# Reads of the first batch and the first down weights, issued earlier in the preparation's store queue

## The chip, the cores and the metric

One core of a Trainium2 chip runs the kernel. The metric is the device time of one execution in microseconds; the time before is the median of three runs. A batch is one of eight sequences of 512 tokens.

## What is computed

Each of 8 x 512 tokens of width 128 is normalised; a two-way state-space layer (forward and reversed, 256 channels, 16 states) and a mixture of 16 experts (the best 4 a token) are both computed from the normalised token and added to it. Cut to what matters:

```python
xn = _layernorm(x)
# state-space layer, for each direction
u = silu(causal_conv(x_part(xn)));  x_dbl = einsum('bdl,kd->bkl', u, xproj_w)
delta = softplus(dtproj(x_dbl[:, :r]) + dt_bias);  Bm, Cm = x_dbl[:, r:r+n], x_dbl[:, r+n:]
dA = exp(einsum('bdl,dn->bdln', delta, A));  dBx = einsum('bdl,bnl,bdl->bdln', delta, Bm, u)
h = associative_scan(a1*a2, a2*b1 + b2)          # along the sequence
y = (einsum('bdln,bnl->bdl', h, Cm) + Dp*u) * silu(z)
# experts
topv, topi = top_k(-dist2(xn, keys) + xn @ rw + rb, 4);  w = softmax(topv)
fused = sum_k w[k] * (gelu(xn @ w1[topi[k]] + b1) @ w2[topi[k]] + b2)
return x + out_proj(y_forward + y_backward) + fused
```

## The kernel before

The program has a start, a preparation and a main loop. Five engines run their own instruction lists and meet at semaphores.

The **preparation** goes through the eight batches. For each batch b, TensorE projects, ScalarE applies the activations, and VectorE does the convolution and the softplus; the results (delta, du = delta times u, gate, skip, parts, and the rows of C) are stored to DRAM, because all batches don't fit on the chip. Each result has one staging buffer, which the next batch writes again when the store has landed. GpSimd meanwhile scatters the token rows to the slots of their experts by 128 indirect DMAs (L804).

The **main loop** goes through the eight batches again, 32 steps (q) each. VectorE does a product (L1556) and two scans (L1568) a step, GpSimd multiplies the states by the rows of C (L838), TensorE fills PSUM banks with B (L1305, L1308), sums the states (L1244) and runs the experts' tiles; ScalarE makes the decays (L1068) and empties banks. A batch reads what the preparation stored: `early` is delta, du and parts, `late` is gate and skip. There are two places for each (par 0 and 1); batch 0 uses place 0, which the preparation doesn't use. The experts have a ring of two for their weights: w1 (up, `read_w1`) and w2 with b2 (down, `read_down`). The memory of w1 is also the staging buffer of the gate (`zg`), so it is free only when the last gate is stored; that of w2 is not used before.

SyncE (SP) issues all reads and stores, in the order of its program, so each one is issued only when all before it are. In the preparation that order is `store_prepared(b)` for b = 0 to 6: C of batch b+1, skip of b, gate of b+3, parts of b+1, delta of b, du of b, each after a wait for its writer. Then come `read_ahead` (L574: the early and the late reads of batch 0) and `read_weights` (L587: w1, w2 and b2 of the tiles 0 and 1, each after loading the tile's expert from the chip's memory, L551), then `store_prepared(7)` with skip, delta and du of the last batch, then `read_first` (L595: after the scatter has landed, the rows and tags of the tiles 0 and 1), a wait for `prepared`, and four reads of C rows (`read_c`, L654).

What the start of the main loop waits for: VectorE signals `prepared` (L1535) and goes on when the stores of gate, C, parts and delta of all eight batches have landed and du is made. TensorE waits for the last skip (`skip_sb`) and parts and for batch 0's early reads, then turns du (L1212) and B (L1217); ScalarE copies the results (L974), scales (L986) and makes decays, for which it waits for `decay_free` (VectorE's L1514); TensorE's first fills (L1305, L1308) follow. ScalarE copies skip to its staging buffer at L943, after TensorE's skip matmuls (L1185) and the landing of the store of the skip before. In step 1 TensorE turns the rows of tile 0 (L1258), and in step 0 GpSimd needs the first C rows.

Of the kernel before, what the change touches and what calls it, by code (L numbers as in the profile page):

```python
# [15 lines left out]
BATCH, L = 8, 512  # L16
# [39 lines left out]
W_RING = 2  # L56
# [202 lines left out]
PREP_STORES = ("gate_out", "c_out", "parts_out", "skip_out", "delta_out", "du_out")  # L259
# [34 lines left out]
def build_kernel(nc, x_in, consts_in, chan_in, inw_in, xproj_in, dtw_in, outw_in,  # L294
                 route_in, b2_in, w1_in, w2_in, out):
    with ExitStack() as ctx:
# [3 lines left out]
        def sem(name):  # L300
            return ctx.enter_context(nc.semaphore(name))
# [172 lines left out]
        s = {n: sem(n) for n in names.split()}  # L474
# [27 lines left out]
        def _(sp):  # L502
# [34 lines left out]
            def read_early(b, par, k):  # L537
                dst, src = early_reads(par)[k]
                sp.dma_start(dst, one(src, b)).then_inc(s[f"early_in{par}"], 16)

            def read_late(b, par, k):

                if k < NH:
                    sp.dma_start(gate[:, par, k, :, :], gate_d[bass.ds(b, 1)].rearrange("e p (t h c) -> (e p) h t c", t=TPB, h=NH)[:, k])\
                        .then_inc(s[f"late_in{par}"], 16)
                else:
                    sp.dma_start(skip[:, par, k - NH, :], skip_d[bass.ds(b, 1)].rearrange("e p (h l) -> (e p) h l", h=NH)[:, k - NH])\
                        .then_inc(s[f"skip_in{par}"], 16)

            def expert_of(tile):  # L550
                return sp.value_load(tile_expert[0:1, bass.ds(tile, 1)], min_val=0, max_val=E - 1)  # L551
# [4 lines left out]
            def read_w1(tile, slot):  # L556
                e = expert_of(tile)
                sp.dma_start(w1[:, slot, :], w1_in[bass.ds(e, 1)].rearrange("e p n -> (e p) n")).then_inc(w1_in_s[slot], 16)
# [9 lines left out]
            def read_down(tile, slot):  # L568
                e = expert_of(tile)
                sp.dma_start(w2[:, slot, :, :].rearrange("p f d -> p (f d)"),  # L570
                             w2_in[bass.ds(e, 1)].rearrange("e p n -> (e p) n")).then_inc(w2_in_s[slot], 16)
                sp.dma_start(b2[0:3, slot, :], b2_d[bass.ds(e, 1)].rearrange("e k d -> (e k) d")).then_inc(w2_in_s[slot], 16)

            def read_ahead():  # L574

                for n in PREP_STORES:
                    sp.wait_ge(s[n], 16)
                sp.wait_ge(s["slots_zeroed"], 16 * ZERO_DMAS)
                sp.wait_ge(s["acc_filled"], 16 * ACC_DMAS)
                for k in range(3):  # L580
                    read_early(0, 0, k)

                sp.wait_ge(s["gate_out"], 16 * BATCH)
                for k in range(2 * NH):
                    read_late(0, 0, k)

            def read_weights():  # L587

                sp.wait_ge(s["b2_out"], 16)
                sp.wait_ge(s["experts_ready"], 1)  # L590
                for j in range(W_RING):
                    read_w1(j, j)
                    read_down(j, j)

            def read_first():  # L595

# [23 lines left out]
            def store_prepared(b):  # L620
                if b + 1 < BATCH:
                    store_c(b + 1)
                store(b, skip_d, skip_p.rearrange("p h l -> p (h l)"), "skip_sb", "skip_out")
                if b + 3 < BATCH:
                    store_gate(b + 3)
                if b + 1 < BATCH:
                    store_parts(b + 1)
                store(b, delta_d, pos_part.rearrange("p q l -> p (q l)"), "delta_ready", "delta_out", ND)
                store(b, du_d, du_p.rearrange("p q l -> p (q l)"), "du_ready", "du_out", ND)
# [12 lines left out]
            store_gate(2)  # L642
            for b in range(BATCH - 1):
                store_prepared(b)
            read_ahead()
            read_weights()
            store_prepared(BATCH - 1)
            read_first()
            sp.wait_ge(s["prepared"], 1)
# [1039 lines left out]
```

## Time and profile before

| | us |
|---|---|
| median of 3 runs | 1097.3 |
| lowest and highest | 1092.97, 1101.39 |
| span of the profiled execution | 1105.0 |
| VectorE busy in it | 1030.1 (93%) |
| ScalarE busy | 940.6 (85%) |
| TensorE (matmul) busy | 932.6 (84%) |
| GpSimd busy | 909.1 (82%) |
| moved by DMA | 228.87 MB, mean 207 GB/s |

The span is that of one execution with the profiler on; it is 7.7 us above the median of the runs. Times in the rows count from the span's start. In a timeline a row with xN is N instructions merged, from the first one's start, with their time in all; in brackets stands how long the engine was idle before it and what ended that. "issue" there means that the profile found no releaser, "remote" that the releasing event belongs to no instruction it knows. The ends of matmuls are modelled.

### The profile page before, as it was taken

The numbers are of one execution on the slowest core, as the hardware profiler recorded it, in microseconds if no ns is written. First come the engines' busy times: TensorE is split into PE (matmuls) and PEld (weight loads), VectorE is DVE, ScalarE is ACT, GpSimd is POOL, SyncE is SP. The second block draws the span as 40 slices with busy tenths as digits, with TensorE's granted clock in tenths as the row PEclk, the third lists the DMA queues.
The fourth block names the chain that finished last, engine by engine and source line by source line (L and its number), as shares of the span: only waits on it lengthen the run. The fifth ranks groups of instructions, "written<-read, shape, count | busy, mean of one in ns | idle before, by whom it ended". The sixth has DMA issues, their size and how long they took to land.

```text
span 1105.0 us, 21807 instructions
## 1 busy us (share of the span) xinstructions
PE 932.6 (84%) x5794; PEld 735.3 (67%) x5866; DVE 1030.1 (93%) x1361; ACT 940.6 (85%) x1755; POOL 909.1 (82%) x567
## 2 busy tenths in 40 slices
PE   4569889955789898999998989989889989988894
PEld 2133333324678787878887877878778878877783
DVE  7789999777999999999999999999999999988897
ACT  3247999968899989999998999999989989988960
POOL 4178888863679999999999899989999999989762
PEclk9778888677999999999999999999999999998997
DMA  9945655689556767687778767776876787666668
GB/s 306 371 147 204 249 197 187 254 282 309 169 166 172 215 193 212 175 238 195 187 201 212 203 166 211 195 208 174 233 200 178 210 216 203 161 171 164 174 137 240
DMA packets 153108, 228.87 MB, mean 207 GB/s; under 512 B 36301, under 2 KB 98029, under 8 KB 147701
## 3 DMA queue, kind: packets, MB, share of 16 engines
q1 hardware_dynamic: 125844, 208.39, 58.6%
q0 software_dynamic: 27136, 19.02, 12.3%
q8 instruction: 51, 0.84, 0.3%
q14 instruction: 77, 0.62, 0.2%
HBM read 161.84 MB, written 69.64 MB: 209 GB/s over the span
## 4 chain that ended last, share of the span: by engine, by line
POOL 34%; issue 30%; ACT 14%; PE 10%; DVE 6%; DMA 3%; SPq 2%; POOLq 1%; ACTq 0%; DVEq 0%; another core or an unknown queue 0%
POOL arena L838 19%; POOL acc_d L823 14%; ACT arena L1068 3%; PE ps L1176 2%; PE ps L1160 2%; ACT arena L986 1%; DMA acc_d<-yrows,tags 1%; PE ps L1145 1%; ACT arena L1007 1%; DVE arena L1464 1%; ACT arena L937 1%; ACT arena L933 1%; ACT arena L1036 1%; PE ps L1244 1%; PE ps L1273 1%
## 5 line engine op out<-in xcount | busy, mean ns | idle before, releaser
L1568 DVE TENSOR_TENSOR_SCAN arena<-arena,ps 128x512 f32<-128x512 f32 x512 | 599.0, 1205 | 1.8 <-issue 0.8
L838 POOL TENSOR_TENSOR arena<-arena 128x1024 f32<-128x1024 f32 x246 | 527.2, 2469 | 54.6 <-DVE arena L1568 34.9
L1068 ACT ACTIVATE arena<-delta,a_neg 128x511 f32<-128x511 f32 x512 | 341.3, 728 | 2.6 <-DVE arena L1568 2.4
L823 POOL DMA_INDIRECT acc_d<-yrows,tags x160 | 252.7, 1579 | 45.2 <-issue 37.1
L1244 PE MATMUL ps<-ident,arena 128*128 128x128 f32 x2048 | 270.2, 275 | 4.6 <-DVE arena L1576 3.4
L1556 DVE TENSOR_TENSOR ps<-du,ps 128x512 f32<-128x512 f32 x352 | 233.2, 679 | 25.9 <-issue 9.5
L1244 PEld LDWEIGHTS ps<-ident,arena 128*128 128x128 f32 x2048 | 232.9, 142 | 15.1 <-DVE arena L1576 3.8
L804 POOL DMA_INDIRECT slots_d<-arena,pos x128 | 149.2, 1165 | 40.2 <-issue 35.8
L1273 PE MATMUL ps<-w,arena 128*128 128x128 f32 x1248 | 173.9, 282 | 3.4 <-ACT arena L1036 3.0
L1273 PEld LDWEIGHTS ps<-w,arena 128*128 128x128 f32 x1248 | 153.7, 192 | 12.8 <-issue 3.8
L1265 PE MATMUL ps<-rowsT,w 128*128 128x256 f32 x640 | 154.7, 385 | 7.8 <-ACT arena L1018 7.5
L986 ACT ACTIVATE arena<-arena 128x256 f32<-128x256 f32 x320 | 145.5, 511 | 0.0
L1265 PEld LDWEIGHTS ps<-rowsT,w 128*128 128x128 f32 x640 | 119.0, 193 | 26.7 <-ACT arena L1018 9.1
L1007 ACT ACTIVATE arena<-ps,w 128x256 f32<-128x256 f32 x312 | 123.8, 477 | 7.2 <-PE ps L1265 6.4
L1305 PE MATMUL ps<-ident,arena 128*128 128x128 f32 x640 | 95.0, 278 | 19.8 <-DVE arena L1568 16.0
L1305 PEld LDWEIGHTS ps<-ident,arena 128*128 128x128 f32 x640 | 74.3, 143 | 25.1 <-DVE arena L1568 18.0
L1013 ACT ACTIVATE yrows<-ps,tags 128x128 f32<-128x128 f32 x160 | 49.8, 365 | 46.7 <-PE ps L1275 21.0
L1036 ACT ACTIVATE arena<-arena 128x1024 f32<-128x1024 f32 x78 | 79.1, 1054 | 0.2
L1464 DVE SCALAR_TENSOR_TENSOR arena<-arena,chan 128x512 f32<-128x512 f32 x96 | 64.7, 742 | 0.0
L1258 PE MATMUL ps<-ident,rows 128*128 128x128 f32 x160 | 33.5, 291 | 36.6 <-ACT arena L1007 22.3
L1160 PE MATMUL ps<-arena 128*104 128x512 f32 x64 | 48.8, 934 | 5.3 <-DVE arena L1523 5.3
L1258 PEld LDWEIGHTS ps<-ident,rows 128*128 128x128 f32 x160 | 18.3, 142 | 51.9 <-ACT arena L1007 22.0
(154 smaller groups left out, 915.2 us busy)
## 6 DMA issues: line engine op xcount, KB each, us to landing
arena<-c_d SPq DMA_DIRECT2D x128, 512.0 KB
w<-w_dram SPq DMA_DIRECT2D x80, 258.0 KB
w<-w_dram SPq DMA_DIRECT2D x80, 256.0 KB
rows<-slots_d SPq DMA_DIRECT2D x80, 130.0 KB
slots_d<-delta SPq DMA_DIRECT2D x5, 2015.0 KB, 18.7
delta_d<-arena SPq DMA_DIRECT2D x8, 1024.0 KB
du_d<-delta SPq DMA_DIRECT2D x8, 1024.0 KB
delta<-delta_d SPq DMA_DIRECT2D x8, 1024.0 KB, 6.6
```

What stands on the lines that cost most here:

```text
L804: pool.indirect_dma_start(slots_d, bass.IndirectOffsetOnAxis(ap=pos[:, t * TOPK + k:t * TOPK + k + 1], axis=0), xn[:, t, :], None).then_in ...
L823: pool.indirect_dma_start(acc_d[j % W_RING], bass.IndirectOffsetOnAxis(ap=tags[:, j, a, 0:1].bitcast(I32), axis=0), yrows[:, j % W_RING, a ...
L838: nc.gpsimd.tensor_tensor(state[:, q % H_RING], state[:, q % H_RING], c_rows[:, r % C_RING], ALU.mult).then_inc(s["prod_done"], 1)
L986: last = nc.scalar.activation(scaled_du[scaled_slot(g, j)][:, t, :], duT[:, par, t, :], ACT.Identity, scale=bT[:, par, t, n:n + 1])
L1007: last = nc.scalar.activation(hidden[hidden_slot(b, j)][:, c, :], bank[:, f * S:(f + 1) * S], ACT.Identity, bias=w1[:, j % W_RING, FF + c: ...
L1068: nc.scalar.activation(decay[:, q % DA_RING, j, lo:lo + L - 1], delta[:, par, dh, lo:lo + L - 1], ACT.Exp, scale=a_neg[:, dh, 2 * g + j:2 ...
L1244: last = nc.tensor.matmul(y_ps[:, h, t * P:(t + 1) * P], state[:, q % H_RING, j, t * P:(t + 1) * P], ident[:, :], is_transpose=True, start ...
L1265: last = nc.tensor.matmul(bank[:, f * S:(f + 1) * S], w1[:, slot, c * P:(c + 1) * P], rowsT[:, :], start=True, stop=True)
L1273: nc.tensor.matmul(bank[:, a * P:(a + 1) * P], kept[:, c, a * P:(a + 1) * P], w2[:, slot, c, :], start=c == 0, stop=False)
L1305: last = nc.tensor.transpose(bank[:, t * P:(t + 1) * P], scaled_du[scaled_slot(g, j)][:, t, h * P:(h + 1) * P], ident[:, :])
L1556: nc.vector.tensor_tensor(b_ps[:, ROW[q, j], j, :], du[:, par, q % DH, :], b_row, ALU.mult)\
L1568: nc.vector.tensor_tensor_scan(state[:, q % H_RING, j, way], decay[:, q % DA_RING, j, way], b_ps[:, ROW[q, j], j, way], 0.0, ALU.mult, ALU ...
```

## The change

The early reads of batch 0 are issued behind the stores of batch 1 (`store_prepared(1)`), the late reads behind those of batch 2, and the reads of the first two tiles' w2 and b2 behind those of batch 3. The two reads of w1 stay where they are, ahead of the stores of batch 7, with the wait for all gates in front of them. The waits in front of the reads are cut to what each needs. No read and no store is added or taken away.

```diff
             def read_ahead():
 
-                for n in PREP_STORES:
+                for n in ("parts_out", "delta_out", "du_out"):
                     sp.wait_ge(s[n], 16)
                 sp.wait_ge(s["slots_zeroed"], 16 * ZERO_DMAS)
                 sp.wait_ge(s["acc_filled"], 16 * ACC_DMAS)
                 for k in range(3):
                     read_early(0, 0, k)
 
-                sp.wait_ge(s["gate_out"], 16 * BATCH)
+            def read_behind():
+
+                sp.wait_ge(s["gate_out"], 16)
+                sp.wait_ge(s["skip_out"], 16)
                 for k in range(2 * NH):
                     read_late(0, 0, k)
 
-            def read_weights():
+            def read_down_weights():
 
                 sp.wait_ge(s["b2_out"], 16)
                 sp.wait_ge(s["experts_ready"], 1)
                 for j in range(W_RING):
+                    read_down(j, j)
+
+            def read_up_weights():
+
+                sp.wait_ge(s["gate_out"], 16 * BATCH)
+                for j in range(W_RING):
                     read_w1(j, j)
-                    read_down(j, j)
...
             for b in range(BATCH - 1):
                 store_prepared(b)
-            read_ahead()
-            read_weights()
+                if b == 1:
+                    read_ahead()
+                elif b == 2:
+                    read_behind()
+                elif b == 3:
+                    read_down_weights()
+            read_up_weights()
             store_prepared(BATCH - 1)
             read_first()
```

## Rows read from the trace of the kernel before

**Rows 1.** The page, shares of the chain that ended last, by engine.
```profile
POOL 34%; issue 30%; ACT 14%; PE 10%; DVE 6%; DMA 3%; SPq 2%; POOLq 1%; ACTq 0%; DVEq 0%; another core or an unknown queue 0%
```

**Rows 2.** Busy time by stretch: stretch, length, PE, PEld, DVE, ACT, POOL, clock, DMA share, GB/s.
```profile
60.00:251.00 191.00, 154.97 (x320) 62.92 (x320) 167.10 (x216) 152.85 (x167) 148.82 (x135) 0.80 0.60 218
258.00:1065.00 807.00, 721.04 (x5188) 634.94 (x5258) 782.60 (x868) 754.58 (x1522) 723.90 (x396) 0.99 0.72 195
```

**Rows 3.** Timeline of SP, 232 to 255 us: start, duration, line, operation, out<-in.
```profile
232.31 0.71 SPq L606 DMA_DIRECT2D du_d<-delta  x1
234.50 0.70 SPq L539 DMA_DIRECT2D delta<-delta_d  x1
...
252.00 0.35 SPq L606 DMA_DIRECT2D delta_d<-arena  x1
252.47 0.78 SPq L606 DMA_DIRECT2D du_d<-delta  x1
253.60 0.94 SPq L561 DMA_DIRECT2D rows<-slots_d  x1
```

**Rows 4.** The chain that ended last in order of time, where the main loop begins.
```profile
258.60 4.93 DMA arena<-c_d
...
263.69 2.56 POOL arena L838 x2
```

**Rows 5.** Timeline of DVE, 247 to 261 us.
```profile
247.19 2.35 DVE L1505 TENSOR_TENSOR delta<-arena 128x1024 f32<-128x1024 f32 x2
249.50 0.17 DVE L1514 MEMSET arena<- 128x2 f32 x8
257.74 0.70 DVE L1556 TENSOR_TENSOR ps<-du,ps 128x512 f32<-128x512 f32 x1 [8.07 <-issue]
258.35 2.33 DVE L1568 TENSOR_TENSOR_SCAN arena<-arena,ps 128x512 f32<-128x512 f32 x2
```

**Rows 6.** Timeline of PE, 232 to 255 us.
```profile
232.02 6.40 PE L1185 MATMUL ps<-arena 128*128 128x512 f32 x8
248.06 1.97 PE L1212 MATMUL ps<-ident,du 128*128 128x128 f32 x8 [9.65 <-ACT gatedT L943]
...
253.30 1.09 PE L1305 MATMUL ps<-ident,arena 128*128 128x128 f32 x4 [3.15 <-ACT arena L986]
```

**Rows 7.** Timeline of ACT, 235 to 257 us.
```profile
235.32 1.02 ACT L923 ACTIVATE arena<-ps 128x1024 f32<-128x1024 f32 x1 [3.10 <-remote]
...
240.45 1.14 ACT L937 ACTIVATE arena<-du,fit_bias 128x1024 f32<-128x1024 f32 x1
246.99 1.01 ACT L943 COPY gatedT<-ps 128x1024 f32<-128x1024 f32 x1 [5.40 <-remote]
...
253.06 3.76 ACT L1068 ACTIVATE arena<-delta,a_neg 128x511 f32<-128x511 f32 x6
```

**Rows 8.** Timeline of POOL, the last indirect DMA of the scatter.
```profile
243.29 0.96 POOL L804 DMA_INDIRECT slots_d<-arena,pos  x1 [0.31 <-issue]
```

**Rows 9.** Busy time by stretch, as in rows 2, before the main loop.
```profile
230.00:235.00 5.00, 5.00 (x8) 1.80 (x7) 2.30 (x3) 2.17 (x3) 4.09 (x4) 0.57 1.04 413
235.00:240.00 5.00, 3.41 (x5) 1.03 (x4) 1.10 (x2) 4.65 (x5) 3.78 (x5) 0.75 0.98 268
240.00:245.00 5.00, 0.00 (x0) 0.00 (x0) 4.69 (x5) 1.59 (x2) 3.34 (x4) 0.59 1.02 398
```

**Rows 10.** Timelines of SP, DVE and ACT in the middle of the preparation.
```profile
131.99 0.39 SPq L606 DMA_DIRECT2D delta_d<-arena  x1
142.59 0.33 SPq L614 DMA_DIRECT2D c_d<-arena  x1
...
140.71 1.21 DVE L1489 SCALAR_TENSOR_TENSOR arena<-arena,du 128x1024 f32<-128x1024 f32 x1
...
158.46 0.56 ACT L905 COPY arena<-ps 104x512 f32<-104x512 f32 x1
```

**Rows 11.** Busy time by stretch, as in rows 2, behind the stores of batch 1.
```profile
140.00:142.00 2.00, 0.94 (x3) 0.12 (x1) 1.92 (x3) 2.00 (x3) 1.70 (x2) 1.00 0.20 71
```

## The prediction

> **What bounds the kernel now.** I read first the busy time by stretch. In the main loop VectorE works 782.60 of 807 us, 97% [rows 2]; in the preparation from 60 us on it works 167.10 of 191 us. So the time is VectorE's two stages and what lies between them. The chain that ended last names GpSimd first, with 34% [rows 1], but in the main loop GpSimd works 723.90 of 807 us [rows 2] and takes what VectorE hands it, so both would have to move for the end to move.
>
> Between the stages is a gap. VectorE's timeline ends the preparation with L1514 at 249.50 + 0.17 = 249.67 and begins step 0 with the product L1556 at 257.74, 8.07 us later [rows 5]. The reader is to see there that nothing computes. The timeline of SP says what it waits for: delta of batch 7 is complete when L1505 starts at 247.19 [rows 5], but its store is issued at 252.00 [rows 3], since SP is held up with the reads of batch 0 from 234.50 and then the weights. `prepared` needs that store landed: 252.00 to 257.74 is 5.7 us, which fits. TensorE had the first fills ready before: its L1305 ran at 253.30 [rows 6], the second fill some 0.4 us behind its end, about 254.8. GpSimd's first product is at 263.69, released by C rows issued at 258.60 that took 4.93 us [rows 4]. So the landing of the last delta store sets VectorE's start, and SP's list sets GpSimd's.
>
> **The change part by part.** Stores, reads and bytes stay the same in number; SP's order changes.
>
> *Taken from 234 to 251 us:* the early reads (2 x 1024 KB + 256 KB = 2.36 MB), the late ones (4 x 256 KB = 1.05 MB), and w2 with b2 (0.52 MB). What stays ahead of the stores of batch 7 is two w1 reads, 0.53 MB. SP ends the stores of batch 6 with du at 232.31 + 0.71 = 233.0 [rows 3]; From there to 252.0 it issues 13 reads today (3 early, 4 late, 2 each of w1, w2 and b2), 1.5 us each. The two w1 reads are 3 us at that pace, and even at twice that, for the expert loads, it is free by 239 and waits for batch 7. Its stores then go out when they are ready: delta at about 247.4 instead of 252.00, du at 249.7 instead of 252.47.
>
> *Landing of that delta store.* 1.05 MB at the 413 GB/s of rows 9 is 2.5 us, the lower bound; the upper one is the 5.7 us of today, with the skip store and weights ahead of it. With nothing ahead, as the skip would have left earlier, I take 3.6, nearer the lower: landed at 251.0. VectorE also needs two decays for its first scan; these follow L1514 at 249.67 at 3.76 / 6 = 0.63 each [rows 7], about 251.0, where today's first scan is at 258.35. VectorE therefore starts at about 251.0 instead of 257.74: **6.7 us earlier** (4.6 with the upper bound, 7.3 with the lower, where the decays decide).
>
> The Trainium skill (DMA: Bandwidth & Descriptors, Anatomy of one DMA) gives each DMA a fixed cost of about 2.0 us beside its bytes. An estimate by that page is 2.0 + 2.5 = 4.5 us for this store instead of 3.6, a start at 251.9 and 5.8 us instead of 6.7. No row shows the store alone.
>
> *The other gate* is TensorE and ScalarE. From ScalarE's skip copy L943 at 246.99 to the second fill at 254.8 is 7.8 us [rows 6, 7]. That copy started late: ScalarE was free at 240.45 + 1.14 = 241.6, the skip matmuls' modelled end is 232.02 + 6.40 = 238.4, and yet it waited 5.40 us, to 246.99, for an event that the profile can't name. The like happened at 235.32 (3.10 us). Both lie where the DMA share is 0.98 to 1.04 [rows 9]. If the reads' traffic causes the second, it goes with them: copy at 241.6, second fill at 249.4, no gate. If it stays, fills come at 254.8 as today, and the gain is 257.74 - 254.8 = **2.9 us**.
>
> *The runs against the profiled execution.* Its span is 1105.0, 7.7 above the median and 3.6 above the slowest run. The two nameless waits are 8.5 us together, so the timed runs may lack them. Without them in either kernel VectorE ends the preparation 3.1 us earlier, at 246.6. In the kernel before, the DMAs then set the landing: from 230 us on 2.10 MB of stores of batch 6, 2.36 + 1.05 + 1.05 MB of reads, and 1.57 MB of skip and delta of batch 7 are 8.1 MB, at the 413 GB/s of the first window 19.7 us, at the mean of rows 9 (360) 22.6: landed at 249.8 to 252.7, middle 251.2. In the changed kernel: delta issued at 244.3, landed at 247.9. Gain **3.3 us** (1.9 to 4.8).
>
> Three states of one mechanism give 2.9, 3.3 and 6.7. I take 4.5, between, as I can't tell which state a timed run is in: 1097.3 - 4.5 = **1092.8**. Against the profiled execution it would be 1105.0 - 6.7 = 1098.3.
>
> *Does the gain reach the end?* GpSimd must come too. SP issues du at 249.7, then four reads of rows and tags, at 1.2 us each today (253.60 to 258.60 [rows 3, 4]) or 0.5 where the queue is short: C rows issued at 252 to 255 instead of 258.60, landed 4.9 later, at 257 to 260 instead of 263.5. Its lag behind VectorE is 5.95 us today and 6 to 9 then; over the 256 steps VectorE needs 3.06 a step and GpSimd 2.83 [rows 2], and VectorE has eight state buffers (24 us) before it feels the lag. Rows of tile 0, needed in step 1, are issued 4.1 us ahead of VectorE's start today and 1.0 then, but behind 1.05 MB of stores instead of 2.62, which at 413 GB/s is 3.8 us less. I count no loss for them; the bound is the 3.1. The last indirect DMA of the scatter starts at 243.29 [rows 8]; SP asks for it at 250, so that wait is free up to a landing of 6 us. From there the main loop is the same work.
>
> *Added to the preparation:* at 133 us, behind du of batch 1, 2.36 MB; at 154, behind batch 2, 1.05 MB; at 175, behind batch 3, 0.52 MB with two expert loads. SP has nothing to issue from there to the next C store, 142.59 for the first [rows 10], and the new waits are for stores of batch 0, landed long before. The cover is idle DMA time: at 140 to 142 us the share is 0.20 [rows 11]. Gate, parts, delta and du of batch 1 and the reads are 5.2 MB, 12.7 us at 413 and 14.6 at 360; counted from the delta store at 131.99, with all of it still to come, they drain by 144.7 to 146.6. The C store of 142.59 is held up by up to 4 us; its buffer is written again at 158.46 [rows 10]. The tightest is delta of batch 1: issued at 131.99, landed 5.7 later at 137.7, awaited at 140.71 [rows 10], 3.0 us to spare. The reads stand behind it; were the engines to share evenly, it would take another 2.5 us and still be in time. Cost: nothing; without that cover, 0 to 2 us.
>
> **The rivals.**
> 1. *Nothing arrives.* Something else behind the start takes it: the rows, or the C rows for GpSimd, which only gain 3.6 of it at their upper cost. For it: the chain runs through GpSimd [rows 1, 4]. Against: VectorE's 97%. Time 1097.3, within 1.
> 2. *Both nameless waits are in the timed runs, and both go.* The preparation then also ends 3.1 earlier: 6.7 + 3.1 = 9.8, time 1087.5. Against: the first, at 235.32, is over before most of the reads are underway.
> 3. *The waits move with the reads (the slower side).* If reads of 3.4 MB beside running matmuls are what delays TensorE's release, it will happen at batch 2 and 3 instead, where VectorE has no idle time to hide it. Price: 3.1 + 8.6 (238.4 to 246.99) = 11.7, less 6.7: 5.0 slower, 1102.3. It decides once the waits put into the preparation pass 6.7 us. Against: the timelines of the middle of the preparation, where each batch's stores run beside the same matmuls, have no such wait.
>
> **How the numbers follow.** Forecast 0.70, rival 1 0.13, rival 2 0.08, rival 3 0.09. The forecast's own range is 1097.3 less 1.9 to 7.3: 1090.0 to 1095.4, and the median of three runs that spread from 1092.97 to 1101.39 is itself uncertain by some 3 us: 1087 to 1098.5. The range for 8 in 10 takes in rival 1 and part of 2: 1085 to 1100. A measurement here can tell about 1% from no change, 11 us. Faster by over that (below 1086.3) needs rival 2 and luck: 0.05. Slower by over that (above 1108.3) needs rival 3 at more than twice its price: 0.03. Within: 0.92.
>
> **What would show it.** Right: early reads at about 133 us; delta of batch 7 stored within 0.3 us of being ready; VectorE's gap after L1514 down from 8.07 to 1 to 5 us; first C rows issued by 255; preparation ending at 246 to 250 as before; the main loop as long as before. Wrong: VectorE idle before L1489 or the convolution in batches 2 to 4 (stores landing late), L943 waiting for a nameless event there, the gap still 8 us, or GpSimd's lag growing until VectorE waits.

## The result, and the profile after

| | before | after |
|---|---|---|
| median of 20 runs, us | 1096.66 | 1092.11 |
| lowest and highest | 1092.97, 1101.44 | 1087.96, 1096.31 |
| ratio, 95% interval | | 0.995 [0.9936, 0.9963] |
| span of the profiled execution | 1105.0 | 1091.1 |
| idle between the stages (VectorE) | 8.07 | 2.02 |

The change makes the kernel about 5 us faster, 0.5%; the interval is clear of no change, though the step is under the 1% that the prediction set out to tell. The medians differ by 4.6 us, the ratio's interval is 4.1 to 7.0 us. The forecast was 1092.8.

Timeline of DVE after, 238 to 247 us (start, duration, line, operation, out<-in, idle before it and its releaser), where the preparation ends; lines have moved by 13, so it answers [rows 5]:

```profile
238.63 2.35 DVE L1518 TENSOR_TENSOR delta<-arena 128x1024 f32<-128x1024 f32 x2
240.93 0.17 DVE L1527 MEMSET arena<- 128x2 f32 x8
243.13 0.70 DVE L1569 TENSOR_TENSOR ps<-du,ps 128x512 f32<-128x512 f32 x1 [2.02 <-issue]
243.74 2.32 DVE L1581 TENSOR_TENSOR_SCAN arena<-arena,ps 128x512 f32<-128x512 f32 x2
```

The gap behind the memsets is 2.02 us instead of 8.07. The releaser is the same unnamed one ("issue"). The timeline of SP after, 223 to 247 us, answers [rows 3]:

```profile
225.45 0.33 SPq L614 DMA_DIRECT2D du_d<-delta  x1
227.06 2.10 SPq L558 DMA_DIRECT2D w<-w_dram  x2
234.01 0.35 SPq L614 DMA_DIRECT2D skip_d<-gatedT  x1
238.81 0.35 SPq L614 DMA_DIRECT2D delta_d<-arena  x1
241.07 0.33 SPq L614 DMA_DIRECT2D du_d<-delta  x1
243.26 0.41 SPq L561 DMA_DIRECT2D rows<-slots_d  x1
```

SP is free from 229.2 us and waits for its writers. Delta's last write ended at 238.7, its store is issued at 238.81. The view of the DMAs issued from 238.5 to 239.5 us (KB, us from issue to landing) says when it is down:

```profile
delta_d<-arena SPq DMA_DIRECT2D x1, 1024.0 KB, 3.9
```

238.81 + 3.9 = 242.7, and VectorE goes on at 243.13. The main loop is as long as before, by stretches of 807 us from the first product on (columns of [rows 2]):

```profile
60.00:243.00 183.00, 146.60 (x326) 60.85 (x325) 162.16 (x210) 155.90 (x175) 144.90 (x132) 0.85 0.65 236
243.00:1050.00 807.00, 728.26 (x5262) 635.11 (x5263) 783.29 (x868) 757.13 (x1528) 723.72 (x396) 0.99 0.73 196
```

VectorE works 783.29 of 807 us, against 782.60 in [rows 2]. From first product to end it is 1091.1 - 243.13 = 848.0 us, against 1105.0 - 257.74 = 847.3. (Over the twelve executions below this stretch took 842.6 us in ballast_b to 851.3 in stores_first_b, and 844.2 in reads_twice, whose start is that of before. One profile thus can't show a gain of a few us at the end; the timed ratios have to.)

The two spans differ by 13.9 us, three times what the runs show, and only 6.05 of it is the gap. The rest lies in the execution of before that was profiled; a second one, below, has a span of 1095.2.

### The profile page after: what moved, and what is told of

Same layout as the page of the kernel before. It is cut to its first block and busy times, and to the rows that moved or that the text cites. A ratio compares the mean times of both kernels' runs of the same rounds, so it can differ in the third digit from the quotient of the medians.

```text
span 1091.1 us, 21878 instructions
## 1 busy us (share of the span) xinstructions
PE 932.0 (85%) x5866; PEld 732.8 (67%) x5866; DVE 1029.2 (94%) x1361; ACT 940.0 (86%) x1755; POOL 907.3 (83%) x567
## 5 line engine op out<-in xcount | busy, mean ns | idle before, releaser
L1321 PE MATMUL ps<-parts,sel 128*128 128x512 bf16 x176 | 59.3, 390 | 12.9 <-DVE arena L1581 12.9
```

## The experiments

Each row of the table is one kernel. Gain is 1097 times one less the ratio. "Ready" is the end of delta's last write by VectorE, "landing" the time from issue to landing of batch 7's delta store, "gap" VectorE's idle time ahead of its first product, "next 60" its idle time in the 60 us from that product on; all are from the profiled execution. For the kernels called split it is the second half of that store, whose issue is the end of SP's merged row for both less 0.33.

| kernel | ready | issued | landing | landed | VectorE starts | gap | next 60 | ratio [95%] | gain us |
|---|---|---|---|---|---|---|---|---|---|
| before_again | 237.6 | 241.37 | 6.1 | 247.5 | 247.86 | 7.87 | 0.5 | 0.9989 [0.997, 1.0008] | 1.2 |
| reads_twice | 239.0 | 242.01 | 7.1 | 249.1 | 249.50 | 8.02 | 0.5 | 0.9997 [0.9972, 1.0021] | 0.3 |
| ballast_b | 238.9 | 242.02 | 7.8 | 249.8 | 250.19 | 8.89 | 0.5 | 0.9998 [0.9976, 1.002] | 0.2 |
| stores_first | 241.7 | 241.80 | 6.7 | 248.5 | 248.87 | 4.78 | 1.5 | 0.9994 [0.9969, 1.002] | 0.7 |
| stores_first_b | 238.7 | 238.83 | 6.6 | 245.4 | 245.85 | 4.73 | 3.7 | 0.9994 [0.9975, 1.0013] | 0.7 |
| rest_alone | 239.1 | 239.18 | 5.9 | 245.1 | 245.83 | 4.34 | 1.7 | 0.997 [0.995, 0.999] | 3.3 |
| ballast_behind | 239.3 | 239.35 | 4.9 | 244.3 | 244.67 | 3.02 | 3.9 | 0.9985 [0.9967, 1.0003] | 1.6 |
| early_alone | 238.0 | 238.11 | 4.7 | 242.8 | 243.16 | 2.70 | 0.0 | 0.9951 [0.993, 0.9972] | 5.4 |
| after | 238.7 | 238.81 | 3.9 | 242.7 | 243.13 | 2.02 | 0.5 | 0.995 [0.9936, 0.9963] | 5.5 |
| after_again | 239.2 | 239.26 | 3.9 | 243.2 | 243.57 | 1.95 | 1.9 | 0.9918 [0.9889, 0.9946] | 9.0 |
| split (second half) | 242.2 | 242.26 | 2.7 | 245.0 | 245.35 | 0.78 | 0.5 | 0.9932 [0.9903, 0.9961] | 7.5 |
| split_b (second half) | 240.2 | 240.31 | 2.7 | 243.0 | 243.37 | 0.76 | 0.1 | 0.9946 [0.9924, 0.9968] | 5.9 |

ballast, which has no row here for want of a usable profile, is told below. In eleven of the twelve VectorE starts 0.4 us behind that landing, whatever else was moved. The exception is rest_alone with 0.7. The gap is thus three terms: how late the store is issued, how long it takes to land, and some 0.4 us, less the 2.3 to 2.4 us that VectorE still works behind delta's last write (for before_again 3.8 + 6.1 + 0.4 - 2.4 = 7.9). The expectations on record were written before these landings were read, and speak of a second gate at TensorE that this table leaves little room for.

The gap alone doesn't tell the gain; the gap and the next 60 us together do. Windows of DVE from the first product on, in before_again, stores_first_b and ballast_behind (stretch, length, VectorE busy, clock, DMA share, GB/s):

```profile
247.86:307.86 60.00, 59.51 (x67) 0.88 0.64 204
```
```profile
245.85:305.85 60.00, 56.26 (x63) 0.85 0.68 213
```
```profile
244.67:304.67 60.00, 56.10 (x63) 0.81 0.67 222
```

Where the rows of tile 0 go out too late for VectorE's start, it loses up to 3.4 us there that before_again doesn't lose: TensorE waits for them (to 251.52 in ballast_behind, 251.58 in stores_first_b), and the fills of step 2 stand behind them in its list. Gap and next 60 together fall below those of before_again by 5.9 us in after, 5.7 in early_alone, 2.3 in rest_alone, 1.4 in ballast_behind, 2.1 and -0.1 in the two of stores_first, 7.1 and 7.5 in the two of split, and -0.1 and -1.0 in reads_twice and ballast_b. All lie inside the interval of the timed gain but after_again, with 4.5 against 9.0 (5.9 to 12.2, from six runs).

### The kernel before, profiled once more

No edit. It tells the nameless waits of [rows 7] apart from the kernel.

> The kernel before, unchanged, profiled and timed once more. It asks whether the trace of before was typical. Ratio 1.000 with an interval of about 0.0015 either way. Theory A (the reads' traffic delays TensorE's release): the wait ahead of the skip copy L943 is there again, 3 to 6 us with no releaser named. Theory B (those waits were of that one execution): TensorE's release comes with the matmuls' end, the copy starts by 0.5 us after ScalarE is free, and the idle time of VectorE after L1514 is by so much longer or the preparation's end earlier. By either, the gap before the main loop is 5 to 9 us and the last delta store is issued 3 to 6 us after delta is made.

The timelines of DVE, ACT and SP, 224 to 248 us:

```profile
231.81 0.99 ACT L943 COPY gatedT<-ps 128x1024 f32<-128x1024 f32 x1
...
239.81 0.17 DVE L1514 MEMSET arena<- 128x2 f32 x8
247.86 0.70 DVE L1556 TENSOR_TENSOR ps<-du,ps 128x512 f32<-128x512 f32 x1 [7.87 <-issue]
...
225.58 1.13 SPq L539 DMA_DIRECT2D parts<-parts_d  x1
226.75 2.25 SPq L544 DMA_DIRECT2D gate<-gate_d  x2
229.05 5.65 SPq L547 DMA_DIRECT2D skip<-skip_d  x2
235.82 0.36 SPq L558 DMA_DIRECT2D w<-w_dram  x1
...
241.37 0.35 SPq L606 DMA_DIRECT2D delta_d<-arena  x1
```

L943 runs without a wait, and so does what comes before it; none of the twelve profiles of the table has a wait of ScalarE or TensorE put down to "remote" between 60 us and the main loop. The 3.10 and 5.40 us were that one execution's, which has a third such wait, of 2.65 us, at 86.87. The gap is there all the same, 7.87 us. SP's list sets it: delta was ready at 237.6 and issued 3.8 us later, the reads ahead of it having taken SP from 224.7 on. And the early reads, issued by 226.7, land late; the timeline of PE, 225 to 245 us, shows what waits for them:

```profile
238.22 1.94 PE L1212 MATMUL ps<-ident,du 128*128 128x128 f32 x8 [7.66 <-DMA parts<-parts_d]
...
244.73 1.06 PE L1305 MATMUL ps<-ident,arena 128*128 128x128 f32 x4 [0.22 <-issue]
```

VectorE's first product needs the fill L1308 between the two of L1305, so TensorE is ready before the second L1305 at 244.73 has run, some 3 us ahead of VectorE's start at 247.86; it isn't what ends the gap here.

The head of the preparation differs too. L1489 of batch 2 starts at 133.19 here and at 140.71 in [rows 10]; in the other executions that can be read it was 133.7 to 138.4. So of 13.9 us between the first two spans, 6.35 are the head (140.71 - 134.36), 6.05 the gap, and 2.2 the stretch from there to the memset's end (108.96 - 106.74), where the nameless waits were; 0.7 went the other way in the main loop.

### Only the early reads moved

```diff
                 if b == 1:
                     read_ahead()
-                elif b == 2:
-                    read_behind()
-                elif b == 3:
-                    read_down_weights()
+            read_behind()
             read_up_weights()
+            read_down_weights()
```

> Only the early reads (2.36 MB) are issued behind the stores of batch 1; late reads, w1, w2 and b2 stay ahead of the last stores. Theory (what counts is how much stands ahead of the last delta store): of the 3.94 MB that the change moves, 60% are gone, so some 2.5 to 3 us of the 4.6 us, ratio 0.9975, and SP still issues ten transfers there. Rival (SP's issue time counts, not the bytes): three of eleven moved issues are gone, 1 to 1.5 us. Rival (early reads are what TensorE's turn of du waits for): nearly the whole 4.6 us, 0.995.

Gain 5.4 us (3.1 to 7.7), the whole of the change's. With only three of the reads gone SP is through its list in time, and delta is stored at 238.11, as soon as it is made. That is neither the theory's 2.5 to 3 us by bytes nor the rival's 1 to 1.5 by issues: without the 2.36 MB in front of them the other issues are shorter too (the two skip reads took SP 2.14 us instead of 5.65), and a lateness can't fall below nothing. The third figure, nearly the whole, came true, but not by its mechanism, since TensorE's turn of du was no gate in before_again. It lands 0.8 us later than in the changed kernel (4.7 against 3.9), with the weights' reads just ahead of it, which is the 0.7 us that the gap is longer.

### Only the late reads and the down weights moved

```diff
-                if b == 1:
-                    read_ahead()
-                elif b == 2:
+                if b == 2:
                     read_behind()
                 elif b == 3:
                     read_down_weights()
+            read_ahead()
             read_up_weights()
```

> The other half alone: the late reads behind the stores of batch 2, w2 and b2 behind those of batch 3, the early reads at their old place. By bytes 1.57 of 3.94 MB are gone, 1.8 us, ratio 0.998; by issues eight of eleven, 3 us or more, 0.997; if TensorE's turn of du waits for the early reads, 0.5 us at the most, 1.000.

Gain 3.3 us (1.1 to 5.5). The timelines of SP, PE with its weight loads (PEld), and DVE:

```profile
239.18 0.35 SPq L614 DMA_DIRECT2D delta_d<-arena  x1
...
239.00 1.94 PE L1224 MATMUL ps<-ident,du 128*128 128x128 f32 x8 [5.88 <-DMA parts<-parts_d]
...
244.88 0.15 PEld L1320 LDWEIGHTS ps<-parts,sel 128*128 128x128 bf16 x1
...
245.52 1.06 PE L1317 MATMUL ps<-ident,arena 128*128 128x128 f32 x4 [0.22 <-issue]
...
245.83 0.69 DVE L1568 TENSOR_TENSOR ps<-du,ps 128x512 f32<-128x512 f32 x1 [4.34 <-PE ps L1317]
```

Delta is issued on time here too, yet the gap is 4.34 us. The view of DMAs issued from 239 to 239.7 us says why: the store takes 5.9 us behind the 2.36 MB of early reads.

```profile
delta_d<-arena SPq DMA_DIRECT2D x1, 1024.0 KB, 5.9
```

Its landing would have let VectorE start at 245.1 + 0.4 = 245.5. It started at 245.83. The early reads also held up TensorE's turn of du, to 239.00, and with it the fill that the first product needs, L1320 (L1308 in the kernel before). Its weights are loaded at 244.88, its matmul is missing in the trace; where it is there, it stands 0.43 us ahead of the fill behind it and takes 0.63, so here it would be over at 245.52 - 0.43 + 0.63 = 245.7 (an estimate). So TensorE is the last gate in this kernel, by some 0.3 us. The gains of the two halves, 5.4 and 3.3, add up to more than the whole, 5.5: each takes away the same lateness of 3.8 us, and moving the early reads takes most of the longer landing as well.

### The order of before, with the last stores ahead of the weights

```diff
             read_ahead()
-            read_weights()
             store_prepared(BATCH - 1)
+            read_weights()
```

> Before's order but for one swap: the weights (w1, w2, b2 of the first two tiles) are read behind the stores of batch 7, not ahead of them. If the landing of the last delta store sets VectorE's start, it is issued within 0.5 us of delta's being made, and the gap after L1514 shrinks by 3 to 5 us; ratio 0.996 to 0.998, with the early and late reads in place. If the bytes already in the queue set the landing, not the issue, the gain is that of 1.05 MB, 2 to 2.5 us. If the main loop swallows an earlier start, 1.000. The weights arrive later; w1 is needed in step 3, some 9 us in, so it costs nothing.

> Before's order with the weights behind the stores of batch 7, once more. Its first profile had a gap of 4.8 us instead of 7.9, and from the middle of the preparation to the main loop 3.1 us less than before_again, but its timed ratio was 0.9994 with an interval from 0.9969 to 1.0020. If the gap is what counts, the ratio is 0.997; if rows and tags, which now stand behind the weights, cost what the start gains (VectorE waited 1.1 us in step 1 or 2), 0.998 to 1.000.

Both times the gap is 3.1 us shorter, and both times the gain is 0.7 us with no change inside its interval (-2.2 to 3.4, then -1.4 to 2.7). Two things are to be seen. First, DVE's timeline of stores_first_b names TensorE's fill for the gap; the timeline of PE has the fill that the product needs:

```profile
244.26 0.63 PE L1308 MATMUL ps<-parts,sel 128*128 128x512 bf16 x1
...
245.85 0.70 DVE L1556 TENSOR_TENSOR ps<-du,ps 128x512 f32<-128x512 f32 x1 [4.73 <-PE ps L1305]
```

The expectations took it at its word. But that fill was over at 244.89, 0.96 us ahead of the product, and those of L1305 are for the first scan and the next step. The delta store of 238.83 landed 6.6 us later, at 245.4, 0.4 us ahead of the product as everywhere else. So the name doesn't tell what came last (in split, below, neither).

Second, the 3.1 us aren't kept. The weights are now ahead of rows, tags and C rows. The timelines of SP, DVE and POOL:

```profile
238.83 0.34 SPq L606 DMA_DIRECT2D delta_d<-arena  x1
...
248.10 0.31 SPq L572 DMA_DIRECT2D b<-b_d  x1
248.78 0.41 SPq L561 DMA_DIRECT2D rows<-slots_d  x1
...
250.76 2.22 SPq L654 DMA_DIRECT2D arena<-c_d  x4
...
252.73 1.29 DVE L1556 TENSOR_TENSOR ps<-du,ps 128x512 f32<-128x512 f32 x2 [1.13 <-PE ps L1308]
...
256.26 5.91 POOL L838 TENSOR_TENSOR arena<-arena 128x1024 f32<-128x1024 f32 x3 [16.77 <-DMA arena<-c_d]
```

The first C rows go out 4.9 us behind VectorE's start, where before_again issued them at 247.80, 0.06 ahead of it; rows follow VectorE's start by 2.9 us instead of preceding it by 4.9. GpSimd begins 10.4 us behind VectorE. VectorE idles 3.7 us in the next 60 us, against 0.5 in before_again: the whole of the 3.1 us is spent there. In the profile of stores_first it is 1.5 us, which leaves 2.1; the main loop is longer by 4.0 and 1.0 us (851.3 and 848.3 against 847.3).

So the gain became a new wait, in one execution all of it, in the other a third.

### The reads of before made twice

All reads of the change are issued in the preparation (`read_besides`, behind the stores of batches 1, 2 and 3) and once more at their old place.

```diff
             for b in range(BATCH - 1):
                 store_prepared(b)
+                read_besides(b)
+            sp.wait_ge(s["extra"], 16 * 11)
             read_ahead()
```

> Before's order, and the 3.94 MB that the change moves are also read, into the same places, behind the stores of batches 1, 2 and 3; at their old place everything is read again. It costs the moved reads' presence in the preparation and leaves their old place as it was. Theory (idle DMA time covers them): ratio 1.000 within 0.0015, VectorE's rhythm of 21.1 us a batch unchanged there. Rival 3 of the prediction (the reads hold TensorE or a store up in mid-preparation): each batch that they touch gets longer, 3 to 8 us in all, ratio 1.003 to 1.007, with VectorE idle ahead of its convolution or of L1502.

Ratio 0.9997: 3.9 MB more in the middle of the preparation cost nothing that the runs can tell (-2.3 to 3.1 us). Timelines of DVE, the first instruction of this kind in batch 2 and in batch 3, in reads_twice, then in before_again and after:

```profile
134.57 1.22 DVE L1518 SCALAR_TENSOR_TENSOR arena<-arena,du 128x1024 f32<-128x1024 f32 x1
...
155.71 1.22 DVE L1518 SCALAR_TENSOR_TENSOR arena<-arena,du 128x1024 f32<-128x1024 f32 x1
```
```profile
133.19 1.21 DVE L1489 SCALAR_TENSOR_TENSOR arena<-arena,du 128x1024 f32<-128x1024 f32 x1
...
154.32 1.21 DVE L1489 SCALAR_TENSOR_TENSOR arena<-arena,du 128x1024 f32<-128x1024 f32 x1
```
```profile
134.36 1.21 DVE L1502 SCALAR_TENSOR_TENSOR arena<-arena,du 128x1024 f32<-128x1024 f32 x1
...
155.48 1.22 DVE L1502 SCALAR_TENSOR_TENSOR arena<-arena,du 128x1024 f32<-128x1024 f32 x1
```

21.14, 21.13 and 21.12 us a batch. These rows reach as far as batch 3. The down weights come in behind it, but from the first of these instructions to the end of the memsets the preparation takes 106.9 us in reads_twice, 106.8 in before_again and 106.7 in after. Rival 3, that the waits move into the preparation, would have shown here.

### Reads put ahead of the last delta store, and behind it

Five reads, 1.31 MB together, into places that nothing needs, in the changed kernel: two halves of gate, two of skip, and parts, all to place 1.

```diff
+                if b == BATCH - 1:
...
+                    sp.dma_start(parts[:, 1, :, :].rearrange("p d l -> p (d l)"), one(parts_d, 0)).then_inc(s["extra"], 16)
                 store(b, delta_d, pos_part.rearrange("p q l -> p (q l)"), "delta_ready", "delta_out", ND)
```

> The changed kernel, with five reads (gate, skip and parts of batch 0 into the unused places, 1.31 MB) put right ahead of the last delta store once delta is made. The early reads are in since long, so TensorE's side is ready. If the landing of the delta store sets VectorE's start and the main loop passes it on: 1.31 MB at 410 GB/s, the landing 3.2 us later, gap 2.0 + 3.2 = 5.2 us, the time 3 to 4 us above the changed kernel's, ratio to before about 0.998. If only the early reads' landing counted, the gap stays 2 to 3 us and the ratio 0.995.

The profiled execution of this kernel took 4968.9 us, with TensorE at a fraction of its pace (1040 ns a matmul of the state sums, 275 in before), and says nothing on the gap. It wasn't every engine, as the next expectation has it: VectorE's scans took 1208 ns, in before 1205. Its timed runs gave 1.0025 [1.0001, 1.0049], 2.7 us slower than before where 0.998 was expected. It was run again:

> The kernel of ballast once more (1.31 MB of reads right ahead of the last delta store of the changed kernel), since its profiled execution ran at a small fraction of the speed in every engine and can't be read. Its timed runs were about 8 us above the changed kernel's, not the 3 to 4 expected. Theory now: the DMA engines take 3.2 us for the bytes, and SP's five issues, at 0.5 to 1.2 us each in a filled queue, put the delta store itself 2.5 to 5 us later, so gap 2.0 + 5 to 8. Rival: the gap is 5 and the main loop itself is longer by 3 to 4, because rows, tags and C rows come later too.

> The same five reads behind the last delta store, ahead of that of du. Same bytes and issues, same delay for du, rows, tags and C rows, none for delta. If the landing of the delta store alone sets the start: gap 2.0 to 3 us and ratio 0.995, 5 us or more below ballast_b. If the lateness of rows and C rows is what costs: as ballast_b.

The same traffic ahead of the store takes the change's gain away (0.9998, after 1.0025 in ballast; gap 8.89); behind it, it leaves a gap of 3.02 us. The DMAs, first of ballast_b, then of ballast_behind:

```profile
delta_d<-arena SPq DMA_DIRECT2D x1, 1024.0 KB, 7.8
```
```profile
delta_d<-arena SPq DMA_DIRECT2D x1, 1024.0 KB, 4.9
```

Against after_again, the five reads ahead cost 3.0 us in lateness (issued 3.1 after ready instead of 0.1) and 3.9 in landing, 6.9 together, and the gap grew by 6.94. Behind the store only the landing grows, by 1.0, and the gap by 1.07. The gap of ballast_behind is 4.9 us below that of before_again, but the gain is only 1.6 us (-0.3 to 3.6; 0.9985 where 0.995 was expected). Of the difference 3.4 us are idle time in the next 60 us, most of it in step 2 of its DVE timeline, where a fill comes late:

```profile
252.67 1.29 DVE L1577 TENSOR_TENSOR ps<-du,ps 128x512 f32<-128x512 f32 x2 [2.25 <-PE ps L1329]
```

So late rows cost too, once the landing is out of the way: they are issued at 244.45 here, 0.2 us ahead of VectorE's first product. In ballast_b they are issued at 243.19, 7.0 us ahead of it, and nothing is lost behind the start.

### The changed kernel again, and a store in two halves

after_again has no edit. split stores delta and du of batch 7 in halves, each as soon as it is made:

```diff
+                    for d in range(ND):
+                        sp.wait_ge(s[ready], ND * b + d + 1)
+                        sp.dma_start(one(dst, b)[:, d * NH * L:(d + 1) * NH * L],
+                                     src[:, d * NH:(d + 1) * NH].rearrange("p q l -> p (q l)")).then_inc(s[stored], 16)
```

> The changed kernel once more, timed beside the others and profiled again. Ratio 0.995 as on record; gap after VectorE's last preparation instruction 2 to 3 us; from the first product of the main loop to the end 847 to 848 us, as in every trace so far.

> The changed kernel, with the last delta and du stored as two halves by direction, the first as soon as it is made (3.8 us ahead of the second). The second half is 0.52 MB instead of 1.05: its landing 1.2 us sooner, so the gap goes from 2.0 to 1.0 or less, where the two first decays (1.3 us behind the end of the preparation, first scan 0.6 us behind the product) take over: 0.8 to 1.2 us, ratio 0.994. That is about what an interval here can tell; the gap in the profile decides. If C rows for GpSimd were the bound, nothing.

> The changed kernel with the last delta and du stored in halves, once more. Its first profile had a gap of 0.8 us instead of 2.0, ended by TensorE's fill, with the ratio 0.9932 (0.9903 to 0.9961). Expected 0.993 to 0.995; it can't be told from the changed kernel by the interval, so the gap is read again: 0.8 to 1.3 us.

after_again has the gap of after (1.95 us) and the landing of after (3.9). In split the last DMA to wait for has half the size and lands in 2.7 us instead of 3.9, and the gap falls by the same 1.2, to 0.78 and 0.76. The profile names a fill of L1325 here too, but the one that the product needs, L1328, was over at 241.81 in split_b. DMAs of split_b, issued from 240.1 to 241.0 us, and its DVE timeline:

```profile
delta_d<-arena SPq DMA_DIRECT2D x1, 512.0 KB, 2.7
```
```profile
243.37 0.70 DVE L1576 TENSOR_TENSOR ps<-du,ps 128x512 f32<-128x512 f32 x1 [0.76 <-PE ps L1325]
```

Against before it is 0.9932 and 0.9946, gains of 7.5 and 5.9 us; the changed kernel had 0.995 and, from six runs, 0.9918. The 1.2 us are in the traces, twice; the runs can't tell them.

## Why the prediction was right

**The time.** 1092.8 forecast, 1092.11 measured, and the mechanism is the one named: batch 7's delta store was late in SP's list and late in landing, VectorE waited for it, and the main loop passes the gain on. But the 4.5 us were a middle of three figures, and two of those fell; that it came so near is in part luck.

**Landing of that delta store.** Predicted: 4.6 us less late, 3.6 to land instead of 5.7, 6.7 us in the profile. Measured between after and before_again: 3.7 less late, 3.9 to land instead of 6.1 (5.9 together), gap 2.02 instead of 7.87 (5.85), and 6.05 against the profile of before. Two terms were mis-sized: 3.6 was 3.9, and 0.4 us lie between the landing and VectorE's product, 4.3 in all. The estimate by the Trainium skill (DMA: Bandwidth & Descriptors, Anatomy of one DMA), 4.5 us and a gain of 5.8, came nearer than mine. That section gives its 2.0 us for DMAs issued from GpSimd, which the prediction doesn't say; this store is issued from SP. By the two sizes here, 1.05 MB landed in 3.9 us and 0.52 MB in 2.7, so 1.2 for half the bytes and 1.5 for the rest; counted to VectorE's product it is 4.3 and 3.1, and 1.9 for the rest, which agrees.

**The other gate.** This step failed. Its price of 2.9 us hung on the nameless 5.40 us at L943, taken for a delay of TensorE's release by the reads' traffic. before_again has the same reads and no such wait. What the reads do delay is TensorE's turn of du, by landing late themselves (L1212 at 238.22, 7.66 us idle), and their own share in the landing of the delta store. As a gate for VectorE it came last in one kernel alone, rest_alone, by some 0.3 us. Why TensorE's releases came late in the one execution stays open.

**The runs against the profiled execution.** This step failed too. It said that without the nameless waits the gap would be set by 8.1 MB of traffic and the gain be 3.3 us. before_again is that case, and its gap is 7.87 us: the delta store was still issued 3.8 us late. The sum took the span of before, 7.7 us above the median, for a sign of those waits; but 2.2 us of it were theirs and the larger part was a late head, older than batch 2. The figure for either state is therefore the same, about 6 us, and lies inside the runs' 4.1 to 7.0 us. I had halved towards a state that doesn't exist, and 1092.11 came out near 1092.8 because 1097.3 - 6 = 1091.3 is near too.

**Reaching the end.** Right in sum: the timed gain of 5.5 us is that of the gap, and VectorE's idle time in the next 60 us is 0.5 us in after as in before_again. (Behind the first product after and after_again took 848.0 and 847.6 us, before 847.3; but a spread of 842.6 to 851.3 makes that no proof.) C rows went out at 245.57, 2.4 us behind VectorE's start, as the prediction allowed, and GpSimd started 8.2 us behind it. One step was wrong: "that wait is free up to a landing of 6 us". SP is now done with du at 241.4 instead of 253, and stands before the scatter's landing. Waits of SP, in after, then in after_again:

```profile
SPq L607 <- DMA slots_d<-arena,pos: 1.6, 1, 1.6
```
```profile
SPq L607 <- DMA slots_d<-arena,pos: 5.2, 1, 5.2
```

The last scatter started at 238.52 in after and at 244.04 in after_again, where the rows of tile 0 therefore went out only at 247.43. TensorE has them late, and its next fill with them. Timelines of POOL, PE and DVE of after_again:

```profile
244.04 0.96 POOL L817 DMA_INDIRECT slots_d<-arena,pos  x1 [0.30 <-issue]
...
249.89 0.69 PE L1271 MATMUL ps<-ident,rows 128*128 128x128 f32 x2 [8.27 <-DMA tags<-slots_d]
...
251.04 1.29 DVE L1569 TENSOR_TENSOR ps<-du,ps 128x512 f32<-128x512 f32 x2 [1.72 <-PE ps L1321]
```

That is the next bound at this place: of 6 us gained in the gap this execution gives 1.72 back two steps later. [rows 8] had shown the scatter's last issue at 243.29, in a kernel whose SP was done with du at 253.25, ten microseconds behind it.

**The preparation.** Right: nothing. The traffic drained later than worked out (12.7 to 14.6 us from the delta store of 124.79, so by 139.4): the share was still 0.98 at 140 to 142 us and 0.32 behind that. The sum had left out the scatter, C and skip, all of it in the 5.78 MB of 124 to 140 us. Windows of after, 140 to 144 us, the columns of [rows 11] (the work of this execution is 6.35 us earlier by the clock than there):

```profile
140.00:142.00 2.00, 2.00 (x9) 1.50 (x9) 1.90 (x3) 1.99 (x2) 1.39 (x3) 1.00 0.98 384
...
142.00:144.00 2.00, 2.00 (x6) 0.77 (x6) 2.00 (x3) 2.00 (x4) 1.70 (x2) 1.00 0.32 112
```

VectorE's pace of 21.12 us a batch shows that VectorE didn't wait for it.

**The rivals.** 1 (nothing arrives) isn't what happened here; stores_first_b comes nearest to it, where later rows and C rows took back a gap shorter by 3.1 us. 2 and 3 needed the nameless waits to belong to the kernel, and fell with them.

**What would show it.** Early reads at 126.2 us, which with the 6.35 us of the head is 132.6 by the clock of before; delta stored within 0.3 us of ready (0.1), the gap between 1 and 5 us, C rows before 255: all seen, and the main loop unchanged as far as its spread lets one see. The preparation was to end at 246 to 250 as before and ended at 241.10, by the head.

## What to carry to other kernels

A store that the next stage waits for should have nothing ahead of it that it doesn't need: every read there costs it twice, in issue time and in landing time, and behind it the next things in need (here rows and C rows) want the same care. Find the gate by adding issue time and landing time over several kernels, not by the name that one wait carries; and profile the kernel before twice before a wait without a name, or a span far off the median, gets a term in the sum.

## What the hardware showed that I had not expected

- An issue on SP isn't of fixed cost. A DMA on an idle list took 0.33 us (du_d, 225.45, after); two skip reads in a full one took 5.65 us (before_again, 229.05), and tags 1.23 to 1.32 us each there against 0.47 and 0.73 in after.
- Landing grew with what was issued ahead: the same 1024 KB store took 3.9 us alone and 4.7 to 7.8 behind reads. Even reads issued behind it lengthened it, by 1.0 us.
- The head of the preparation is not the same from one execution to the next: over 13 executions the first instruction of VectorE's softplus in batch 2 (L1489) started between 133.2 and 140.7 us, which moves a span by more than the whole change does.
